# A graph-attention kernel: GpSimd's semaphore add at the head of each gather group is taken out

## The chip, the cores and the metric

The kernel runs on one core of a Trainium2 chip. The metric is the device time of one execution in microseconds; the number given for a kernel is the median of its timed runs. A profile is one further execution, recorded by the hardware profiler; its span runs from the first to the last instruction.

The engines are TensorE (PE in the profile, with its weight loads as PEld), VectorE (DVE), ScalarE (ACT), GpSimd (POOL) and SyncE (SP). A name with a q behind it (POOLq, DVEq, SPq) is that engine's sequencer: waits, register work and the issue of transfers.

## The reference, cut to what matters

There are 6,250 nodes with 128 features and 206,250 edges, sorted by destination. Three products of the nodes are taken (Q, K, V), one of the edges (E). Each edge gets a score per head, and the messages are summed per destination:

```python
Qh = (h @ WQ).reshape(N, H, D)          # H = 8 heads, D = 16
Kh = (h @ WK).reshape(N, H, D)
Vh = (h @ WV).reshape(N, H, D)
Eh = (edge_attr @ WE).reshape(-1, H, D)
score = jnp.einsum('ehd,ehd,ehd->eh', Kh[src], Qh[dst], Eh) * inv_sqrt_d
score = jnp.exp(jnp.clip(score, -5.0, 5.0))
msg = Vh[src] * score[:, :, None]
wV = jax.ops.segment_sum(msg, dst, num_segments=N)
Z = jax.ops.segment_sum(score, dst, num_segments=N)
h_out = wV / (Z[:, :, None] + 1e-06)
x = _layernorm(x + h_out)
```

`Kh[src]` and `Vh[src]` are gathers of rows at random. The kernel does them with indirect transfers that GpSimd issues.

## The kernel before, in words

**Groups.** The edges are cut into 403 groups of 512 (G = 403, four tiles of 128 edges each). A first stage computes K and V of all nodes and writes them to `kv_table` in DRAM, and keeps Q on chip in three bf16 parts. The main loop then runs over the groups, eight to a turn; it is unrolled in full, so that each group has its own instructions.

**One group, engine by engine.**
- SP loads the group's 512 source indices into `src_idx` (L272) and its edge features into `attr` (L279). The index buffer has eight slots, `attr` four.
- GpSimd gathers the 512 rows of `kv_table` (1 KB each) into a ring of eight slots, `kv` (RINGS = 8), with four indirect transfers (L436), one for each tile.
- PE turns the edge features (L537, `attr_tr`), turns the one-hot matrix of destinations (L556, `hot_tr`), multiplies the features by WE (L546, `e_mm`), selects Q by the one-hot matrix (L569, `q_sel`) and sums the messages (L580, `sums`).
- ACT copies what PE turned out of PSUM (L726, L733), builds the one-hot matrix (L713, L718) and takes the exponential (L740).
- DVE multiplies K by E (L901, after `e_mm` and `kv_in`), by Q (L906), reduces to scores (L911), clips (L917), forms the messages (L923, `msg_ok`) and adds the sums to the accumulator (L940, after `sums`).

The engines are staggered: while DVE scores group g, PE turns g+2, makes the products of g+1 and sums the messages of g-1.

**The ring.** Group g of the gathers may overwrite its slot when the messages of group g-8 are made. This is the wait on `msg_ok`. The other wait of a group is that its indices have landed (`idx_in`). Both stand in the function `gather`, and behind them a semaphore `go` is raised by one. No instruction waits for `go`.

**Order.** Every engine runs its instructions in program order; what ties them together are the semaphores. After the last group the window sums that are still open are divided, added to x and normalised, and stored.

The names that the steps below touch are: `gather` (L429), its waits at L431 and L433, the add to `go` at L434, the gather itself at L436, and for comparison DVE's two waits ahead of L901 (`e_mm` written first, L898; `kv_in` second, L899) and PE's two ahead of L537 (`attr_in` first, L533; `attrT_ok` second, L535).

Of the kernel before, what the change touches and what calls it, by code (L numbers as in the profile page):

```python
# [32 lines left out]
def past(g, n):  # L33

    return g >= n if isinstance(g, int) else True


def graph_attention_layernorm(nc, x, src, dst, edge_attr, wq, wk, wv, we, out):
# [43 lines left out]
    def edge0(g):  # L82

        return min(g * GROUP, n_edges - GROUP) if isinstance(g, int) else g * GROUP
# [3 lines left out]
    with ExitStack() as ctx:  # L88
# [6 lines left out]
        def sem(name):  # L95
            return ctx.enter_context(nc.semaphore(name))
# [101 lines left out]
        go = sem("go")  # L198
# [199 lines left out]
        @block.gpsimd  # L398
        def _(pool):
            nc.gpsimd.memset(ident[:, :], 0.0).then_inc(id_zero, 1)  # L400
            pool.wait_ge(id_zero, 1)
            nc.gpsimd.affine_select(out=ident[:, :], in_=ident[:, :], compare_op=ALU.not_equal, fill=1.0, base=0,
                                    pattern=[[-1, P]], channel_multiplier=1).then_inc(const_ready, 1)

            def count_up(out, base, n):
                return nc.gpsimd.iota(out, [[1, n]], base=base, channel_multiplier=0,
                                      allow_small_or_imprecise_dtypes=True)


            count_up(iota[:, 0, :], 0, P)  # L410
            count_up(iota[:, 1, 0:HALF], HALF, HALF)
            count_up(iota[:, 1, HALF:P], 0, HALF).then_inc(const_ready, 1)
            nc.gpsimd.iota(table[0:1, FIRST, 0:G - 1], [[GROUP, G - 1]], base=0, channel_multiplier=0)
            nc.gpsimd.iota(table[0:1, FIRST, G - 1:G], [[0, 1]], base=edge0(G - 1), channel_multiplier=0)\
                .then_inc(first_ok, 1)

            nc.gpsimd.iota(table[0:1, OPEN, 0:B_LAST * RINGS].rearrange("a (b u) -> a b u", u=RINGS),
                           [[2, B_LAST], [0, RINGS]], base=2 * (2 - LAG), channel_multiplier=0)
            nc.gpsimd.iota(table[0:1, OPEN, B_LAST * RINGS:G + 1], [[0, G + 1 - B_LAST * RINGS]], base=2 * EARLY,
                           channel_multiplier=0).then_inc(first_ok, 1)  # L420

            pool.wait_ge(prep, 4)
            last = local_rows[:, GC - 1, :]
            nc.gpsimd.affine_select(out=last, in_=last, compare_op=ALU.is_ge, fill=NOT_AN_EDGE,
                                    base=LAST_ROW * 2 * GROUP - REPEATED, pattern=[[1, GROUP]],
                                    channel_multiplier=-2 * GROUP).then_inc(masked, 1)
            nc.gpsimd.memset(acc[:, :, :], 0.0).then_inc(acc_zero, 1)

            def gather(b, u):  # L429
                g = b * RINGS + u  # L430
                pool.wait_ge(idx_in[u], b * 16 + 16)  # L431
                if past(g, RINGS):
                    pool.wait_ge(msg_ok, g - RINGS + 1)  # L433
                pool.sem_inc(go, 1)  # L434
                for t in range(TILES):
                    nc.gpsimd.indirect_dma_start(  # L436
                        out=kv[:, u, t, :], out_offset=None, in_=kv_table,
                        in_offset=bass.IndirectOffsetOnAxis(ap=src_idx[:, u, t:t + 1], axis=0)).then_inc(kv_in[u], 16)

            for i in range(RINGS):  # L440
                pool.wait_ge(kv_stored[i], 16 * len(range(i, CH, RINGS)))
            for u in range(RINGS):
                gather(0, u)
            for b in range(1, B_LAST):
                for u in range(RINGS):
                    gather(b, u)
            for g in range(B_LAST * RINGS, G):
                gather(g // RINGS, g % RINGS)


            pool.wait_ge(table_ok, 1)
            with pool.If(pool.value_load(table[0:1, STRAYS, G:G + 1], min_val=0, max_val=G) > 0):
                with pool.Fori(0, G) as g:
                    nth = pool.value_load(table[0:1, STRAYS, bass.ds(g, 1)], min_val=0, max_val=G)
                    nth_next = pool.value_load(table[0:1, STRAYS, bass.ds(g + 1, 1)], min_val=0, max_val=G)
                    with pool.If(nth_next > nth):
                        pool.wait_ge(s_idx, nth * 16 + 16)
                        pool.sem_inc(go, 1)
                        for t in range(TILES):
                            nc.gpsimd.indirect_dma_start(  # L460
                                out=kv[:, 0, t, :], out_offset=None, in_=kv_table,
                                in_offset=bass.IndirectOffsetOnAxis(ap=src_idx[:, 0, t:t + 1], axis=0))\
                                .then_inc(s_kv, 16)
# [649 lines left out]
```

## Time and profile before

| | us |
|---|---|
| median of 3 runs | 3040.36 |
| the runs | 3032.72 to 3042.60 |
| the profiled execution, device time | 3033.75 |
| its span, first to last instruction | 3031.9 |
| PE busy (share of the span) | 2078.2 (69%) |
| DVE busy | 1490.8 (49%) |
| ACT busy | 1331.4 (44%) |
| POOL busy, 1612 gathers 1530.9 of it | 1539.4 (51%) |
| TensorE's mean granted clock | 0.803 |

No engine is busy for the whole span, so the busy shares alone don't say what bounds the kernel: the order in which the engines wait for each other has to be read. "Issue" as a releaser means that the profile shows nothing that the engine waited for; "remote" and "another core or an unknown queue" mean that the semaphore came from an instruction that the inference did not find.

### The profile page before, as it was taken

To read this page: it belongs to the slowest core of one execution; us is meant where nothing else is said; L and a number is where in the kernel's file an instruction comes from. 1 tells how busy PE (TensorE), PEld (TensorE's weight loads), DVE (VectorE), ACT (ScalarE), POOL (GpSimd) and SP (SyncE) were. 2 spreads that over 40 slices of the span, in tenths; PEclk is the share of its full clock that TensorE was granted. 3 is DMA by queue.
4 is the path that set the end of the run, shared out by engine and by line. 5 is a ranking of instruction groups with operands and counts; after the bars stand their busy time and mean duration, and the time that the engine had idled before them with its cause. 6 is when DMAs were issued, how large, how long until landed. Compare 5 with 4: busy or idle time off the path is not lost.

```text
span 3031.9 us, 50000 instructions
## 1 busy us (share of the span) xinstructions
PE 2078.2 (69%) x14786; PEld 1828.8 (60%) x14787; DVE 1490.8 (49%) x3785; ACT 1331.4 (44%) x3270; POOL 1539.4 (51%) x1628
## 2 busy tenths in 40 slices
PE   6566766776766766667676776676666676767775
PEld 5455656666656665566666666566565566666665
DVE  4444444554454544544445544455445454454546
ACT  2444444444444444444444444444444444444443
POOL 3455554555555555555555555555554555545552
PEclk8688887878787788888777777878878888777778
DMA  7533433433333433334333443333333343433431
GB/s 218 158 110 109 114 111 108 115 111 109 110 110 108 113 111 110 111 109 113 109 111 110 112 112 110 112 106 111 114 109 109 110 112 112 110 110 107 116 109 55
DMA packets 223039, 342.94 MB, mean 113 GB/s; under 512 B 92096, under 2 KB 117672, under 8 KB 222779
## 3 DMA queue, kind: packets, MB, share of 16 engines
q0 software_dynamic: 77376, 211.39, 24.0%
q1 hardware_dynamic: 144827, 128.08, 15.5%
q8 instruction: 132, 2.16, 0.3%
q14 instruction: 128, 1.05, 0.1%
q10 hardware_dynamic: 576, 0.26, 0.0%
HBM read 325.24 MB, written 9.60 MB: 110 GB/s over the span
## 4 chain that ended last, share of the span: by engine, by line
PE 30%; another core or an unknown queue 28%; DVE 18%; issue 16%; DVEq 5%; ACT 3%; DMA 0%; SPq 0%; ACTq 0%
PE psW L580 13%; DVE msg L923 6%; PE psE L546 6%; DVE acc L940 4%; PE psH L556 4%; DVEq L246 3%; PE psQ L569 3%; DVE prod L906 2%; PE psT L537 2%; ACT hot L713 1%; DVE score L911 1%; DVEq L940 1%; ACT hot L718 1%; PE psE L499 1%
## 5 line engine op out<-in xcount | busy, mean ns | idle before, releaser
L436 POOL DMA_INDIRECT kv<-kv_table,src_idx x1612 | 1530.9, 950 | 1437.7 <-issue 1411.3
L580 PE MATMUL psW<-msg,hot 128*128 128x136 f32 x3224 | 647.7, 361 | 379.1 <-DVE msg L923 379.0
L580 PEld LDWEIGHTS psW<-msg,hot 128*128 128x128 f32 x3224 | 555.8, 252 | 419.4 <-DVE msg L923 419.1
L940 DVE TENSOR_TENSOR acc<-psW,acc 64x136 f32 x806 | 239.5, 297 | 1117.3 <-remote 938.8
L726 ACT ACTIVATE attrT<-psT 128x512 f32<-128x512 f32 x403 | 239.8, 595 | 964.9 <-remote 944.7
L569 PE MATMUL psQ<-Qp,hotT 128*128 x4836 | 422.4, 231 | 262.0 <-issue 261.3
L546 PE MATMUL psE<-w_e,attrT 128*128 128x128 f32 x3224 | 539.6, 308 | 89.4 <-issue 85.9
L569 PEld LDWEIGHTS psQ<-Qp,hotT 128*128 128x128 bf16 x4836 | 340.4, 104 | 360.4 <-issue 353.6
L546 PEld LDWEIGHTS psE<-w_e,attrT 128*128 128x128 f32 x3224 | 486.8, 225 | 81.4 <-issue 79.9
L713 ACT ACTIVATE hot<-iota,local 128x128 f32 x1612 | 508.8, 386 | 3.0 <-issue 2.6
L901 DVE TENSOR_TENSOR prod<-kv,psE 128x512 f32<-128x512 f32 x403 | 275.1, 683 | 327.3 <-issue 231.8
L556 PE MATMUL psH<-ident,hot 128*128 128x128 f32 x1612 | 326.3, 337 | 99.0 <-ACT hot L718 51.3
L537 PE MATMUL psT<-ident,attr 128*128 128x128 f32 x1612 | 329.0, 342 | 65.8 <-issue 65.8
L556 PEld LDWEIGHTS psH<-ident,hot 128*128 128x128 f32 x1612 | 219.4, 171 | 199.0 <-ACT hot L718 134.2
L740 ACT ACTIVATE msg<-clipped 128x32 f32<-128x32 f32 x403 | 92.4, 229 | 535.5 <-DVE clipped L917 457.4
L537 PEld LDWEIGHTS psT<-ident,attr 128*128 128x128 f32 x1612 | 263.4, 181 | 74.6 <-issue 74.6
L718 ACT ACTIVATE hot<-hot,one 128x512 f32<-128x512 f32 x403 | 290.9, 722 | 13.0
L906 DVE TENSOR_TENSOR prod<-prod,psQ 128x512 f32<-128x512 f32 x403 | 277.2, 688 | 12.7
L733 ACT ACTIVATE hotT<-psH 128x512 bf16<-128x512 f32 x403 | 239.6, 595 | 90.9 <-PE psH L556 80.4
L923 DVE TENSOR_TENSOR msg<-kv,msg 128x512 f32<-128x512 f32 x403 | 275.9, 685 | 0.3 <-ACT msg L740 0.3
L911 DVE TENSOR_REDUCE score<-prod 128x32 f32<-128x512 f32 x403 | 270.6, 671 | 0.0
L917 DVE TENSOR_SCALAR clipped<-score 128x32 f32<-128x32 f32 x403 | 76.6, 190 | 4.6
(94 smaller groups left out, 362.2 us busy)
## 6 DMA issues: line engine op xcount, KB each, us to landing
attr<-in_edge_attr_dram SPq DMA_DIRECT2D x403, 256.0 KB
kv<-kv_table,src_idx POOLq DMA_INDIRECT x1612
src_idx<-in_src_dram SPq DMA_DIRECT2D x403, 2.0 KB
kv_table<-kv SPq DMA_DIRECT2D x12, 512.0 KB, 3.8
Qp<-Qp SPq DMA_DIRECT2D x23, 192.0 KB
hot<-in_x_dram SPq DMA_DIRECT2D x12, 256.0 KB, 4.5
xT<-in_x_dram SPq DMA_DIRECT2D x8, 384.0 KB
out_dram<-xT SPq DMA_DIRECT2D x45, 64.0 KB
```

The lines of the kernel that those rows point to most:

```text
L436: nc.gpsimd.indirect_dma_start(out=kv[:, u, t, :], out_offset=None, in_=kv_table, in_offset=bass.IndirectOffsetOnAxis(ap=src_idx[:, u, t:t ...
L537: last = nc.tensor.transpose(psT[:, t * P:(t + 1) * P], attr[:, u % ATTRS, t, :], ident[:, :])
L546: last = nc.tensor.matmul(psE[:, u % 2, t * P:(t + 1) * P], attrT[:, u % 2, t * P:(t + 1) * P], w_e[:, :], start=True, stop=True)
L556: last = nc.tensor.transpose(psH[:, t * P:(t + 1) * P], hot[:, g % HOTS, t, :], ident[:, :])
L569: last = nc.tensor.matmul(psQ[:, u % 2, t * P:(t + 1) * P], hotT[:, u % 2, t * P:(t + 1) * P], Qp[:, bass.ds(slot, 1), part, :].rearrange( ...
L580: last = nc.tensor.matmul(psW[:, u % 2, 0:MW], hot[:, g % HOTS, t, :], msg[:, g % MSGS, t, :], start=(t == 0), stop=(t == TILES - 1))
L713: last = nc.scalar.activation(hot[:, g % HOTS, t, :], nodes, ACT.Abs, scale=-1.0, bias=local[:, t, bass.ds(g, 1)])
L718: nc.scalar.activation(slot, slot, ACT.Relu, scale=-1.0 / NOT_AN_EDGE, bias=one[:, 0:1])\
L906: nc.vector.tensor_tensor(prod[:, :], prod[:, :], psQ[:, u % 2, :], ALU.mult).then_inc(keq, 1)
L911: nc.vector.tensor_reduce(score[:, :], prod[:, :].rearrange("p (a d) -> p a d", d=DH), AX.X, ALU.add)\
L923: nc.vector.tensor_tensor(per_head(msg[:, g % MSGS, :, 0:dim]), per_head(kv[:, u, :, dim:2 * dim]), msg[:, g % MSGS, :, dim:MW].unsqueeze( ...
L940: last = nc.vector.tensor_tensor(where, psW[half, u % 2, 0:MW], where, ALU.add)
```

## The change

The line that adds to `go` is removed from `gather`. The two waits ahead of it stay in the program, and so does the order of the four gathers behind them. Nothing else changes; the add in the branch for stray edges at the end of GpSimd's program stays, and that branch isn't entered with these inputs.

```diff
@@ -431,7 +431,6 @@
                 pool.wait_ge(idx_in[u], b * 16 + 16)
                 if past(g, RINGS):
                     pool.wait_ge(msg_ok, g - RINGS + 1)
-                pool.sem_inc(go, 1)
                 for t in range(TILES):
                     nc.gpsimd.indirect_dma_start(
                         out=kv[:, u, t, :], out_offset=None, in_=kv_table,
```

In the program before, both waits are carried by the instruction that adds to `go`, an EVENT_SEMAPHORE of GpSimd's sequencer at L434. Without it the next instruction behind the waits is the group's first gather.

## Rows read from the trace of the kernel before

**Rows 1.** The page's costliest gather line: busy, mean ns, idle before, releaser.
```profile
L436 POOL DMA_INDIRECT kv<-kv_table,src_idx x1612 | 1530.9, 950 | 1437.7 <-issue 1411.3
```

**Rows 2.** Waits of all engines: who waited for whom, us, times, longest.
```profile
POOL kv L436 <- issue: 1411.3, 1611, 34.5
ACT attrT L726 <- remote: 944.7, 197, 5.9
DVE acc L940 <- remote: 938.8, 197, 7.1
```

**Rows 3.** Stretches: length, each engine's busy us (instructions), clock, DMA share, GB/s.
```profile
1508.01:1522.53 14.52, 10.97 (x74) 9.40 (x74) 7.48 (x22) 6.47 (x16) 7.60 (x8) 0.74 0.38 110
1522.53:1537.11 14.58, 11.14 (x74) 9.48 (x74) 7.14 (x21) 6.52 (x16) 7.56 (x8) 0.73 0.38 109
2990.00:3018.80 28.80, 21.68 (x191) 19.63 (x190) 21.73 (x50) 13.51 (x35) 0.00 (x0) 0.94 0.03 11
```

**Rows 4.** Timeline of GpSimd: start, duration, instruction, idle before and its releaser.
```profile
1508.01 0.95 POOL L436 DMA_INDIRECT kv<-kv_table,src_idx  x1 [5.05 <-issue]
1509.26 0.94 POOL L436 DMA_INDIRECT kv<-kv_table,src_idx  x1 [0.30 <-issue]
...
1516.80 0.94 POOL L436 DMA_INDIRECT kv<-kv_table,src_idx  x1 [0.30 <-issue]
1522.53 0.94 POOL L436 DMA_INDIRECT kv<-kv_table,src_idx  x1 [4.79 <-issue]
```

**Rows 5.** Timeline of ACT and DVE behind that burst.
```profile
1519.53 0.60 ACT L726 ACTIVATE attrT<-psT 128x512 f32<-128x512 f32 x1 [4.41 <-remote]
...
1521.07 0.68 DVE L923 TENSOR_TENSOR msg<-kv,msg 128x512 f32<-128x512 f32 x1
```

**Rows 6.** GpSimd's waiting instruction L434, whole run: duration ns min/median/max, first and last start.
```profile
L434 POOLq EVENT_SEMAPHORE  x403: 17/2973/11407, 52.4 to 2977.9; - x135
```

**Rows 7.** The same line in the stretches 53:95, 1513:1522.5 and 1523:1524.
```profile
L434 POOLq EVENT_SEMAPHORE  x7: 17/17/17, 54.4 to 74.2; - x7
...
L434 POOLq EVENT_SEMAPHORE  x1: 7934/7934/7934, 1513.9 to 1513.9; - x1
...
L434 POOLq EVENT_SEMAPHORE  x1: 2677/2677/2677, 1523.7 to 1523.7; - x1
```

**Rows 8.** Lines with two waits, on DVE and on PE: the rows that exist.
```profile
L899 DVEq EVENT_SEMAPHORE  x403: 4/21/174, 115.0 to 3011.5; - x135
...
L901 DVE TENSOR_TENSOR prod<-kv,psE x403: 672/681/690, 115.2 to 3011.6; 128x512 f32<-128x512 f32 x135
...
L535 PEldq EVENT_SEMAPHORE  x402: 51/51/51, 106.6 to 3003.7; - x134
```

**Rows 9.** SP's index loads: duration ns, first and last start; then GpSimd's last gathers.
```profile
L272 SPq DMA_DIRECT2D src_idx<-in_src_dram x403: 327/432/972, 4.3 to 2950.2; - x135
...
2981.74 0.94 POOL L436 DMA_INDIRECT kv<-kv_table,src_idx  x1 [0.30 <-issue]
2983.93 0.94 POOL L436 DMA_INDIRECT kv<-kv_table,src_idx  x1 [1.24 <-issue]
...
2986.42 0.95 POOL L436 DMA_INDIRECT kv<-kv_table,src_idx  x1 [0.30 <-issue]
```

**Rows 10.** Timeline of GpSimd at the start: the first burst's ends and the next gather.
```profile
53.30 1.11 POOL L436 DMA_INDIRECT kv<-kv_table,src_idx  x1 [34.51 <-issue]
...
93.47 0.95 POOL L436 DMA_INDIRECT kv<-kv_table,src_idx  x1 [0.30 <-issue]
120.79 0.94 POOL L436 DMA_INDIRECT kv<-kv_table,src_idx  x1 [26.38 <-DVE msg L923]
```

**Rows 11.** Timeline of GpSimd: a burst with a pause inside, and the next.
```profile
1537.11 0.94 POOL L436 DMA_INDIRECT kv<-kv_table,src_idx  x1 [4.89 <-issue]
...
1542.11 0.94 POOL L436 DMA_INDIRECT kv<-kv_table,src_idx  x1 [0.30 <-issue]
1544.30 0.94 POOL L436 DMA_INDIRECT kv<-kv_table,src_idx  x1 [1.24 <-issue]
...
1549.88 0.94 POOL L436 DMA_INDIRECT kv<-kv_table,src_idx  x1 [2.14 <-issue]
```

## The prediction

> **What bounds the kernel now.** I read the page first. GpSimd's gathers take 1530.9 us, with almost as much idle time between them that no releaser explains [rows 1]. So GpSimd isn't saturated on average, and the question is what its gaps are. The list of waits comes next: ACT and DVE each wait 197 times, some 940 us in all, for something that PE raises (the turned features, the sums), and the releaser isn't found [rows 2]. 403 groups over 197 such waits is two groups a wait, so there is a cycle of two groups. The stretches show it: one cycle is 14.52 to 14.58 us long and holds 8 gathers and 74 matmul records. In the tail, after the last gather, 191 matmul records take 28.80 us. At 37 records a group that is 5.2 groups, so a group takes 7.3 us with gathers in flight and 5.6 without [rows 3]. The clock differs too (0.74 against 0.94).
>
> The timeline gives the cycle's parts. A burst of eight gathers starts at 1508.01 at a pitch of 1.25 us and ends at 1516.80 + 0.94 = 1517.74 [rows 4]. ACT's copy of the turned features, which had waited 4.41 us, starts at 1519.53, and DVE's messages, begun at 1521.07, are ready at 1521.75 [rows 5]. They free a ring slot, and the next burst starts at 1522.53 [rows 4]. So the cycle is
>
> 9.73 (burst) + 1.79 (last gather's end to ACT's release) + 2.22 (to the messages) + 0.78 (to the first gather) = 14.52 us.
>
> PE's semaphores come late in each burst, and come when the burst has drained; why, the trace doesn't say. What matters here is that GpSimd's own time lies on the loop: whatever the head of a burst gains or loses counts once per cycle, 197 times. The span is then 120.8 us to the first gather that waits for messages [rows 10], 2866.6 us of cycles up to 2987.4 [rows 9], and 44.5 us of tail, 3031.9 in all.
>
> **The head of a group before.** The instruction that adds to `go` carries both waits. There is one in each of the 403 groups [rows 6]. In the burst above it stands from 1513.9 for 7.934 us, so it ends at 1521.8, when the messages are ready, and the gather starts 0.7 us behind it [rows 7, 4]. The next one starts at 1523.7, behind four gathers: the sequencer passed four in 1.9 us, 0.47 us each, while the engine needs 1.25 each. So the sequencer runs ahead within a burst, and only the first gather of a burst shows its 0.7 us of start. When both conditions hold already the whole instruction takes 17 ns [rows 7].
>
> **The change, part by part.**
>
> *The add itself.* Nobody waits for `go`. Its cost lies between 0 and the whole satisfied instruction, 17 ns [rows 7]. On 197 burst heads that is 0 to 3.3 us of gain; the other 206 heads are passed while earlier gathers run, and are hidden by them. If that cover were gone they would cost 206 x 0.017 = 3.5 us more.
>
> *Where the waits go.* DVE has two waits ahead of L901. The one written second, `kv_in` at L899, has an EVENT_SEMAPHORE of its own, 403 times; the one written first has no row, so L901 carries it. PE's pair ahead of L537 looks the same: a row at L535, the second [rows 8]. By this pattern GpSimd's second wait, the ring slot, stays an EVENT_SEMAPHORE (now at L433), and the first gather carries the index wait. This is the main point of the forecast: the wait that really ends late, the slot's, still blocks the sequencer before the gather is read, and the 0.7 us of start behind it stay. Only in the first eight groups, which have one wait, the instruction disappears: 8 x 0.017 us, at a time when GpSimd is 26.38 us early [rows 10].
>
> *The wait that the gather now carries.* Queued behind it are the other three gathers of the group and all later ones, and DVE's L901 waits for them. It is satisfied long before: the last index load is issued at 2950.2, and the four gathers of the last group begin at 2981.74 or later, over 31 us behind it [rows 9]. What a carried, satisfied wait costs on a gather no row shows. From below I exclude a gain, since it adds a check. From above I take the dearest satisfied wait by median, PE's 51 ns [rows 8]; DVE's is 21 ns, GpSimd's own 17 [rows 7, 8]. The 51 ns belong to another engine, so I take 17 ns: 197 x 0.017 = 3.3 us, with 0 and 197 x 0.051 = 10.0 as ends. Heads inside a burst are again covered by the gathers that run.
>
> *Sum.* 3033.75 - 3.3 + 3.3 = 3033.75 us for an execution like the profiled one, with ends 3030.4 and 3043.8. That execution lies 6.6 us under the median of the runs, 3040.36. Moved by that, the forecast is 3040.4 us, from 3037.1 to 3050.4; the runs before themselves spread by 10 us, so I widen the case to 3031 at the low end. A change of up to 0.3% (9.1 us) can't be told from none for this kernel.
>
> **A rule of the skill on the carried wait.** The row for GpSimd says that a satisfied wait passes in 17 ns [rows 7]. The Trainium skill, "Advanced Engine Details and Errata", section Miscellaneous Facts, gives 50 to 100 ns for a sequencer's reading of a semaphore. If each burst head paid one such reading more, that would be an estimate of 197 x 0.05 to 0.1 = 10 to 20 us more, 3050 to 3060 us. The trace's satisfied waits, at 17 and 21 ns, don't agree with it.
>
> **The rivals.**
>
> 1. *The ring-slot wait rides on the gather (faster).* If a transfer can carry both waits, or the slot's is the one it carries, the sequencer has read the gather before the slot is free. No row shows a transfer with two waits, so the profile doesn't exclude it; the pattern of two other engines speaks against it [rows 8]. Price: a start like one inside a burst, 0.30 us of gap instead of about 0.74, or one gather's 0.47 us of reading saved: 197 x 0.44 to 0.47 = 87 to 93 us [rows 4, 7]. Then 2948 to 2954 us. What is late next is unchanged, the same loop with a shorter head. The Trainium skill, "Perfetto Trace Analysis", section DMA Instruction — SWDGE (GPSIMD), says that such an instruction is pushed into a wait queue and the sequencer goes on to the next: by that rule, the gain is there whenever the gather carries the slot's wait.
>
> 2. *A gather that carries a wait isn't run ahead (slower).* No row of this trace shows a GpSimd transfer with a wait. If the sequencer reads such a gather only when the one before has ended, the fifth gather of each burst, now hidden, gets the gap of a burst's head: 0.74 instead of 0.30 us, 197 x 0.44 = 87 us, 3127 us. It decides as soon as the carried wait is handled after the read-ahead rather than in it. Against it: the program's other engines carry a wait in every group and run on.
>
> 3. *A small price for each carried wait (slower).* Satisfied waits at PE's 51 ns would give 10.0 us, and twice that 20: 3050 to 3061 us [rows 8].
>
> 4. *A pause inside the burst lets PE through (faster).* One burst in the trace has a pause of 1.24 us behind its fifth gather, and its cycle is 1549.88 - 1537.11 = 12.77 us, shorter by 1.75 than the one shown above, though GpSimd lost 0.94 us [rows 11, 3]. If the carried wait opened such a gap in every burst, 197 x 1.75 = 345 us would go: 2696 us. Nothing says that the gap would be that long.
>
> That the change doesn't do what it says, since the waiting instruction stays, is part of the forecast.
>
> **How the numbers follow.** The forecast, within 0.3%, gets 0.68. Rival 1 gets 0.10, rival 2 0.06, rival 3 0.10, rival 4 0.02; 0.04 is left for what I don't see, half to each side. So faster is 0.10 + 0.02 + 0.02 = 0.14, the same 0.68, slower 0.06 + 0.10 + 0.02 = 0.18. The likeliest case has the range 3031 to 3050. With rival 3, up to 3061, it holds 0.78, just short of 8 in 10, so the range goes down to rival 1 as well, to 2945, and holds 0.88; rivals 2 and 4 are left out.
>
> **What would show each step.** In the profile of the changed kernel: an EVENT_SEMAPHORE of GpSimd at L433, 395 times, with durations like L434's now, and none in the first eight groups (the placement); the first gather of a burst still 0.7 to 0.8 us behind the messages, and the others at a pitch of 1.25 us (the head); the cycle at 14.5 us and 197 waits of ACT for PE (the loop). The prediction is wrong if there is no such instruction and the head's 0.78 us have shrunk (rival 1), if the gap before the fifth gather of a burst is over 0.30 us (rival 2, or 4 if the cycle is then shorter), or if the head grows by 0.05 us or more (rival 3).

## The result and the profile after

| | before | after |
|---|---|---|
| median of 15 runs each, us | 3037.55 | 3030.35 |
| lowest to highest | 3024.01 to 3042.99 | 3020.01 to 3033.79 |
| profiled execution, us | 3033.75 | 3031.2 |
| its span | 3031.9 | 3029.4 |

The ratio is 0.9978, with a 95% interval from 0.9969 to 0.9987. By that ratio the change gives 6.7 us, between 3.9 and 9.4 (the medians are 7.2 apart). The forecast said that nothing would be gained or lost, with 3.3 us as the most that the add could give. A gain was measured, small, but clear of the noise.

The page's line for the gathers and the list of waits, as in [rows 1] and [rows 2] (busy, mean ns and idle in the page's line; us, times and longest in the waits):

```profile
L435 POOL DMA_INDIRECT kv<-kv_table,src_idx x1612 | 1534.2, 952 | 1430.7 <-DVE msg L922 960.9
```
```profile
DVE acc L939 <- remote: 979.6, 196, 7.0
POOL kv L435 <- DVE msg L922: 960.9, 259, 27.2
ACT attrT L725 <- remote: 938.7, 198, 6.1
```

The loop is the same: ACT and DVE wait 196 to 198 times for PE, 939 and 980 us in all. Only the name of GpSimd's releaser is new. Before, the wait lay in the long record of the adding instruction; now the gather is shown to wait for the messages. The waiting instruction over the whole run, to be held against [rows 6] (duration ns min/median/max, first and last start):

```profile
L433 POOLq EVENT_SEMAPHORE  x395: 17/17/17, 121.6 to 2977.3; - x198
```

It stands at L433, 395 times, and not in the first eight groups. Its place was foreseen. Its durations were not: all are 17 ns, at the time when the wait ends, where the old one's record held the wait (2973 ns median). The record of such an instruction says when it ran, but not what it costs. The forecast took its price from such a record.

One burst and the head of the next in the timelines of DVE and GpSimd, to be read beside [rows 4] and [rows 5]:

```profile
1516.53 0.68 DVE L922 TENSOR_TENSOR msg<-kv,msg 128x512 f32<-128x512 f32 x1
```
```profile
1503.47 0.95 POOL L435 DMA_INDIRECT kv<-kv_table,src_idx  x1 [5.03 <-DVE msg L922]
1504.73 0.94 POOL L435 DMA_INDIRECT kv<-kv_table,src_idx  x1 [0.30 <-issue]
...
1508.81 0.95 POOL L435 DMA_INDIRECT kv<-kv_table,src_idx  x1 [0.30 <-issue]
...
1512.55 0.94 POOL L435 DMA_INDIRECT kv<-kv_table,src_idx  x1 [0.30 <-issue]
1517.97 0.94 POOL L435 DMA_INDIRECT kv<-kv_table,src_idx  x1 [4.47 <-DVE msg L922]
```

The messages are ready at 1517.21 and the burst starts at 1517.97, 0.76 us later by these rounded rows. The fifth gather (1508.81), which carries a wait inside the burst, still has its gap of 0.30 us.

Worked out for every burst head in the trace, this distance is so steady that single nanoseconds can be read: 775 ns before and 751 ns after, nine heads in ten within 1 ns. That is 24 ns less in each of 197 heads, 4.7 us. The cycles took 2866.6 us before; after, from 122.3 to the last gather's end at 2984.0, they take 2861.8, 4.8 less. The start (+1.5) and the tail (+0.9) give a part back in this execution. The interval of the 6.7 us holds 4.7. But the agreement is closer than the parts: the regular cycles of eight gathers became 46 ns shorter on average (14.621 to 14.575 us), not 24, which is 9 us, and the few irregular ones, most with a pause like that of [rows 11], saved 12.9 us in all instead of 17.1. So the 24 ns of the head are measured, and that they are all of the gain is not.

### The profile page after: what moved, and what is told of

Its sections match the earlier page's. It is cut to its first block, busy times and chain, and to the rows that moved or that the text cites. A ratio compares the mean times of both kernels' runs of the same rounds, so it can differ in the third digit from the quotient of the medians.

```text
span 3029.4 us, 49992 instructions
## 1 busy us (share of the span) xinstructions
PE 2066.5 (68%) x14786; PEld 1815.6 (60%) x14787; DVE 1492.3 (49%) x3785; ACT 1331.8 (44%) x3270; POOL 1542.7 (51%) x1628
## 3 DMA queue, kind: packets, MB, share of 16 engines
q1 hardware_dynamic: 144827, 128.08, 15.8%
## 4 chain that ended last, share of the span: by engine, by line
PE 34%; another core or an unknown queue 23%; issue 18%; DVE 17%; DVEq 4%; ACT 3%; DMA 0%; SPq 0%; ACTq 0%
PE psW L579 14%; PE psE L545 7%; DVE msg L922 6%; PE psH L555 5%; PE psQ L568 5%; DVE acc L939 3%; PE psT L536 3%; DVEq L246 3%; DVE prod L905 2%; ACT hot L712 2%; DVE score L910 1%; ACT hot L717 1%; DVEq L939 1%; PE psE L498 1%
## 5 line engine op out<-in xcount | busy, mean ns | idle before, releaser
L568 PE MATMUL psQ<-Qp,hotT 128*128 x4836 | 429.8, 230 | 299.0 <-issue 298.3
L545 PE MATMUL psE<-w_e,attrT 128*128 128x128 f32 x3224 | 524.9, 307 | 41.2 <-issue 37.8
L545 PEld LDWEIGHTS psE<-w_e,attrT 128*128 128x128 f32 x3224 | 480.3, 225 | 39.4 <-issue 38.6
```

The lines of the kernel that those rows point to most:

```text
L545: last = nc.tensor.matmul(psE[:, u % 2, t * P:(t + 1) * P], attrT[:, u % 2, t * P:(t + 1) * P], w_e[:, :], start=True, stop=True)
L568: last = nc.tensor.matmul(psQ[:, u % 2, t * P:(t + 1) * P], hotT[:, u % 2, t * P:(t + 1) * P], Qp[:, bass.ds(slot, 1), part, :].rearrange( ...
```

## The experiments

The theory to be tested, A: GpSimd's time in a burst's head counts once a cycle, and the add was 24 ns of it. The rivals: the 24 ns come from the new place of the waits; or the head doesn't set the time at all.

The runs fell on chips of two kinds. On the kind of the first measurement the kernel before takes 3035 to 3076 us and gathers in bursts. On the other kind it takes 2125 to 2130 us, with no bursts. Each result names the kernel before on the same chip. Edits are shown against the kernel before where nothing else is said.

### e1_swap: which wait the gather carries

```diff
-                pool.wait_ge(idx_in[u], b * 16 + 16)
                 if past(g, RINGS):
                     pool.wait_ge(msg_ok, g - RINGS + 1)
+                pool.wait_ge(idx_in[u], b * 16 + 16)
-                pool.sem_inc(go, 1)
```

> The add is gone and the two waits are written in the other order, so that the sequencer's own waiting instruction holds the index wait (long satisfied) and the first gather carries the ring-slot wait. Theory A (the burst head's time is mostly the reading of the gather behind the waiting instruction): the first gather starts about 0.3 us behind the messages instead of 0.75, which takes 197 x 0.44 = 87 us away: near 2945 us. Theory B (the sequencer handles a carried wait itself, before it reads the gather): the head stays at 0.75 us or so and the time is that of the changed kernel, near 3030 us.

Measured: 2993.61 us, before 3075.99, ratio 0.9736 (0.9723 to 0.9749). The head, in DVE's timeline and then GpSimd's:

```profile
1514.03 0.68 DVE L922 TENSOR_TENSOR msg<-kv,msg 128x512 f32<-128x512 f32 x1
```
```profile
1514.99 0.94 POOL L435 DMA_INDIRECT kv<-kv_table,src_idx  x1 [4.09 <-DVE msg L922]
```

1514.71 to 1514.99: 270 ns over all heads, in place of 775. When the gather carries the wait that ends last, most of GpSimd's start lies ahead of it and is no longer paid. How far ahead the sequencer is, the row of the index wait shows (stretch 1514 to 1515.1):

```profile
L433 POOLq EVENT_SEMAPHORE  x1: 17/17/17, 1514.8 to 1514.8; - x1
```

It ends 0.07 us behind the messages and 0.2 us before the gather starts, and by its semaphore it is the index wait of the group behind this one. So the sequencer had passed all four gathers of the group before the slot was free.

The head fell by 505 ns, 99.5 us in 197 cycles, and 82.4 us came out. Other parts moved too (medians, against e2 and e4 below, which ran on the same chip): the fourth gather of a burst takes 1.18 us in place of 0.95, the time from the last gather's end to ACT's release is 1.86 us in place of 2.00, and the bursts with a pause are gone. Why, no run shows. It is faster than both kernels.

### e2_add_first, e3_two_adds, e4_add_behind: where an add stands and how many

```diff
 e2_add_first
+                pool.sem_inc(go, 1)
                 pool.wait_ge(idx_in[u], b * 16 + 16)
...
-                pool.sem_inc(go, 1)
 e3_two_adds
                 pool.sem_inc(go, 1)
+                pool.sem_inc(go, 1)
 e4_add_behind
-                pool.sem_inc(go, 1)
                 for t in range(TILES):
+                    if t == 1:
+                        pool.sem_inc(go, 1)
```

> The add to go stands ahead of both waits: the work is that of the kernel before, but no add lies between the slot's release and the gather. Theory A (the changed kernel's 24 ns are the add on the head of a burst): head 0.751 us as in the changed kernel, ratio to before about 0.998. Theory B (they are the price of one instruction more, or of the semaphore traffic, wherever it stands): head 0.775 us, ratio 1.000.

Measured: 3079.43 us, before 3075.99, ratio 1.0009 (1.0000 to 1.0018). The head is 755 ns.

> The kernel before with a second add to go behind the first, on the head of every group. Theory A (what stands between the release and the gather counts once per burst): the head grows from 0.775 us by the time of one more sequencer instruction, 0.03 to 0.09 us, and the time by 197 times that, 6 to 17 us, ratio 1.002 to 1.006. Theory B (the head of a burst is not on the loop; the changed kernel's gain comes from elsewhere): the head may grow, the time stays, ratio 1.000.

Measured: 3088.12 us, ratio 1.0044 (1.0031 to 1.0058). The head is 853 ns. DVE's and GpSimd's timelines, then the rows of the two adding instructions over the whole run (duration ns min/median/max, first and last start):

```profile
1518.50 0.69 DVE L924 TENSOR_TENSOR msg<-kv,msg 128x512 f32<-128x512 f32 x1
```
```profile
1520.04 0.94 POOL L437 DMA_INDIRECT kv<-kv_table,src_idx  x1 [5.23 <-issue]
```
```profile
L434 POOLq EVENT_SEMAPHORE  x403: 17/2897/11504, 51.5 to 3028.9; - x135
L435 POOLq EVENT_SEMAPHORE  x403: 17/17/17, 51.6 to 3031.6; - x135
```

> The add to go stands between a group's first and second gather; the waits are as in the changed kernel. Theory A (only what stands on the head counts): head 0.751 us, ratio to before 0.998, like the changed kernel. Theory B (an add anywhere in the group costs): ratio 1.000.

Measured: 3068.89 us, ratio 0.9982 (0.9973 to 0.9991). The head is 755 ns.

What follows. A second add, with its row of 17 ns, costs 78 ns in the head: 15.4 us in 197 cycles, and 12.1 were measured in the medians. This speaks for the head being on the loop, and shows that a row's 17 ns isn't its price. e4 behaves like the changed kernel, in head and time. e2 is the miss: its head is as short as e4's, yet nothing was gained. Their regular cycles are 14.73 and 14.72 us (median). They differ in the few bursts that have a pause inside, like that of [rows 11]: these took 14.38 us for eight gathers in e2's profile and 14.17 in e4's. Against a regular cycle these bursts save 6.5 us in e2's profile and 12.0 in e4's, a difference as large as the whole effect. Why they differ stays open, and with it how much of the 6.7 us is the head's: two programs with the same head are 10.5 us apart. An add ahead of the waits, or behind the first gather, is nearly free in the head: 755 ns in e2 and e4, against 751 with none. Only between the last wait and the gather does a second one cost 78 ns.

### e5_add_one_wait and e6_three_waits: the add or the wait

e5 moves the wait for the next group's indices to this group's second gather; the head keeps the add, with the slot's wait alone. e6 has no add, and a third wait that has always been met.

```diff
 e5_add_one_wait
-                pool.wait_ge(idx_in[u], b * 16 + 16)
+                if g == 0:
+                    pool.wait_ge(idx_in[u], b * 16 + 16)
...
+                    if t == 1 and g + 1 < G:
+                        pool.wait_ge(idx_in[(u + 1) % RINGS], (b + (u + 1) // RINGS) * 16 + 16)
 e6_three_waits
+                    pool.wait_ge(kv_stored[0], 16)
-                pool.sem_inc(go, 1)
```

> The wait for a group's indices is moved to the second gather of the group before, so that GpSimd's head of a group is one instruction: the add, which itself carries the only wait left, the one for the ring slot; the gather behind it carries none. From the messages' end to the burst's first gather the kernel before takes 775 ns, the changed one 751 ns. Theory A (the 24 ns are the add: one more instruction between the wait and the gather, whatever it carries): the add is there and the head stays at 775 ns, 0.3% (some 5 us) off the kernel before at most. Theory B (the 24 ns are the second wait: the one behind which an instruction of its own has to stand): the head falls to 751 ns or below, the cycle by the same. Rival C (a satisfied wait carried by a gather costs time of its own, and the add costs more than 24 ns): the head falls below 740 ns, as the gather is free of any wait.

> No add; the head of a group waits for three things instead of two, in the order indices, ring slot, and a first store of the table that has long landed; the gather carries the first, the others stand ahead of it. It measures what one more wait that is already satisfied costs in the head. Theory A (an extra wait that is satisfied is one more instruction in the way, priced as the add is): the head from the messages' end to the first gather is 751 + 24 to 40 = 775 to 790 ns, the cycle of two groups 0.02 to 0.04 us above the changed kernel's 14.55 us, the time 4 to 8 us above it. Rival B (satisfied waits are taken together with the one that ends last and cost nothing): 751 ns and the changed kernel's time. By the second add's price (78 ns) it would be 829 ns.

Measured, both on the kind without bursts: 2132.43 and 2130.28 us, one run each, before 2129.89. There the gathers never stop, and no head is to be seen (e6, timeline of GpSimd):

```profile
1503.19 0.95 POOL L436 DMA_INDIRECT kv<-kv_table,src_idx  x1 [0.30 <-issue]
1504.45 0.95 POOL L436 DMA_INDIRECT kv<-kv_table,src_idx  x1 [0.31 <-issue]
1505.70 0.94 POOL L436 DMA_INDIRECT kv<-kv_table,src_idx  x1 [0.30 <-issue]
```

They ran again on the kind with bursts.

> The same kernel as e5_add_one_wait, which ran on a chip where GpSimd's gathers never stop (0.305 us between two gathers throughout, 2132 us), so that no head of a burst was to be seen. On a chip where the kernel before takes over 3000 us and its gathers come in bursts of eight: Theory A (the 24 ns are the add) 775 ns from the messages' end to the burst's first gather; Theory B (the 24 ns are the second wait) 751 ns or less; Rival C (a carried satisfied wait costs more) below 740 ns. On a chip of the other kind it shows again 0.305 us and the time of the kernel before, whatever stands in the head.

> The same kernel as e6_three_waits (no add, a third wait that is always satisfied). On a chip with bursts: Theory A (an extra satisfied wait is one more instruction in the way) 775 to 790 ns from the messages' end to the first gather and 4 to 8 us over the changed kernel; Rival B (satisfied waits cost nothing) 751 ns. On a chip without bursts: 0.305 us between gathers and the time of the kernel before.

Measured: 3031.09 and 3031.30 us, before 3035.28, one run each; the times can't be told apart, the heads can. e5b's and e6b's, DVE and then GpSimd each:

```profile
1516.51 0.68 DVE L926 TENSOR_TENSOR msg<-kv,msg 128x512 f32<-128x512 f32 x1
```
```profile
1517.97 0.95 POOL L439 DMA_INDIRECT kv<-kv_table,src_idx  x1 [4.52 <-DVE msg L926]
```
```profile
1519.15 0.69 DVE L923 TENSOR_TENSOR msg<-kv,msg 128x512 f32<-128x512 f32 x1
```
```profile
1520.57 0.96 POOL L436 DMA_INDIRECT kv<-kv_table,src_idx  x1 [4.75 <-issue]
```

Neither theory named what came: 785 ns for e5b, 739 ns for e6b. With the two older kernels they make a table in which every entry is the sum of the same two parts (medians, ns; in brackets from the messages' end to the end of the head's last instruction, and from there to the gather):

| the head's instruction | carries two waits | carries one wait |
|---|---|---|
| with an add | before: 775 (41 + 733) | e5b: 785 (52 + 733) |
| without | e6b: 739 (41 + 698) | after: 751 (53 + 698) |

The step from the upper row to the lower is worth 35 ns, all of it behind the instruction. An instruction with one wait answers 11 to 12 ns later than one with two. The change of this case does both: 35 ns gained, 12 lost (775 to 751; the rounding takes the last one). A satisfied third wait makes the head no longer here.

One thing the table doesn't take apart: in the upper row the gather carries no wait, in the lower it carries the index wait. The 35 ns are the add's price less whatever that wait costs on the gather. The add so costs 35 ns or more.

### e9_thin: is it the gathers' data?

Why is there a cycle of 14.5 us at all? In the changed kernel's profile PE's turned features are done long before ACT is released (timelines of PE and ACT):

```profile
1511.30 0.60 PE L536 MATMUL psT<-ident,attr 128*128 128x128 f32 x4
```
```profile
1514.99 0.60 ACT L725 ACTIVATE attrT<-psT 128x512 f32<-128x512 f32 x1 [5.28 <-remote]
```

PE ends at 1511.90 and ACT starts at 1514.99, 3.1 us later, when the burst has drained. The same pair on the other kind of chip (e6):

```profile
1500.67 0.60 PE L537 MATMUL psT<-ident,attr 128*128 128x128 f32 x4
```
```profile
1501.30 0.60 ACT L726 ACTIVATE attrT<-psT 128x512 f32<-128x512 f32 x1
```

0.03 us. The semaphore events in the traces say the same of all that PE raises: in e6 its sums are posted 0.01 us after the matmul's end, all of them. In e1 this holds for one group of each pair; the other's are posted 5.27 us late (median of 198). ACT's and DVE's own posts come after 0.01 us in both. e9 is e1 with narrow rows: it leaves out 15/16 of every row.

```diff
 e9_thin (against e1_swap)
-                        out=kv[:, u, t, :], out_offset=None, in_=kv_table,
+                        out=kv[:, u, t, 0:16], out_offset=None, in_=kv_table.rearrange("n (a d) -> (n a) d", d=16),
```

> As e1_swap, but each gather moves 16 of a row's 256 numbers, from a narrow view of the table: 15/16 of the gathered bytes are left out, and the result is not the reference's. The number of gathers and of their rows, and with them the work of GpSimd in writing descriptors, stay. Theory M (TensorE's posts are held back by the data that the gathers move): with 1/16 of the bytes the posts come through, the gathers no longer come in bursts, the time falls to that of a kernel bound by GpSimd, 2000 to 2150 us. Theory G (they are held back by GpSimd's writing of descriptors, whatever the bytes): bursts of eight and a cycle of 14 us or a little less, 2850 to 2990 us. On a chip without bursts: 0.305 us between gathers, 1.25 us a gather, 2000 to 2130 us by either theory.

Measured: 2959.34 us, before 3035.28 (one run each). The stretch from 1500 to 1600 us shows how little moves (the last two columns are the DMA engines' share and GB/s; e1_swap moves 113 to 115 GB/s in its cycles):

```profile
1500.00:1600.00 100.00, 70.78 (x510) 62.25 (x510) 51.06 (x133) 45.94 (x113) 55.28 (x57) 0.81 0.19 45
```

The bursts of eight stay, the cycle is 14.13 us against 14.31, and the later group's sums are still posted 4.81 us late. So the bytes don't hold PE's posts. What is left is GpSimd's issue of the gathers, as theory G has it, or the number of rows that the transfers handle, which the edit left as it was; no run separates the two.

### e8_pause, e8b_pause, e8c_short: a pause inside the burst

e1 with two small clears of an unused tile on GpSimd, each waiting for the one before, behind every other group's first gather.

```diff
                 for t in range(TILES):
+                    if t == 1 and g % 2 == 0 and g >= RINGS:
+                        for i in range(2):
+                            n = (g - RINGS) // 2 * 2 + i
+                            if n:
+                                pool.wait_ge(go, n)
+                            nc.gpsimd.memset(stray[:, :], 0.0).then_inc(go, 1)
```

> As e1_swap, with a pause written into each burst of 8 gathers behind its fifth gather: two small clears of an unused tile on GpSimd, each waiting for the one before. Theory A (GpSimd's work in a cycle is on the path and adds up): the cycle of 14.31 us grows by what the clears and the pause take, 0.3 to 0.8 us, the time from 2994 to 3050 to 3150 us. Rival (the fourth rival of the prediction: in the pause TensorE's posts, held back while gathers stream, come through, and the chain of the next pair of groups starts earlier; the few bursts with a pause in the kernel before have cycles of 13.8 us per eight gathers, against 14.6): the cycle falls to 13.0 to 13.8 us, the time to 2700 to 2900 us.

Measured without bursts: 2312.74 us, before 2129.89, ratio 1.0856 (1.0831 to 1.0880). GpSimd is the bound there, and pays for the clears.

> The same kernel as e8_pause, which on a chip without bursts took 8.6% more than the kernel before: the two clears take 1.9 us of GpSimd per pair of groups. On a chip with bursts: Theory A (GpSimd's work in a cycle is on the path and adds up): 14.31 + 0.9 to 1.9 = 15.2 to 16.2 us a cycle, 3170 to 3370 us. Rival (in the pause TensorE's held posts come through and the chain of the next pair starts earlier): 12.8 to 13.8 us, 2700 to 2900 us, though GpSimd has more to do.

Measured with bursts: 2910.77 us, before 3035.28 (one run each), 4.1% less, with more work on GpSimd. The gathers now come in groups of many sizes, 13.9 us for eight. Of the 393 posts of PE's sums in its trace 97 fall between two gathers that have the clears between them. The fourth rival of the prediction has its mechanism here.

> As e8b_pause, with the two clears cut to 8 numbers a row each, so that they take little time of their own. On a chip with bursts, Theory P with any pause enough: as much or more gain than e8b (4.1%), 2850 to 2910 us. Rival (the pause of the clears must be long, some 1.1 us between two gathers, for the posts to come through): no gain beyond e1_swap's 2.6%, 2950 to 3010 us. On a chip without bursts: less lost than e8's 8.6%, 0 to 3%.

e8c clears 8 numbers a row in place of 403. Measured with bursts: 2935.58 us, before 3036.8, ratio 0.9674 (0.9652 to 0.9696). The pause, in GpSimd's timeline:

```profile
1507.79 0.95 POOL L441 DMA_INDIRECT kv<-kv_table,src_idx  x1 [0.30 <-issue]
1508.73 0.29 POOL L440 MEMSET stray<- 128x8 bf16 x2
1509.16 0.95 POOL L441 DMA_INDIRECT kv<-kv_table,src_idx  x1
```

It is 0.42 us between two gathers, against 0.30 without it, and even this gives a little over e1's 0.9736, which was measured on another chip. I had expected either the full 4% or nothing; it lies between.

### e7_sums_gate, e7b_sums_gate, e10_gate_even: a stop until PE has posted

```diff
 e7_sums_gate (against e1_swap)
-                    pool.wait_ge(msg_ok, g - RINGS + 1)
+                    pool.wait_ge(sums, g - RINGS + 1)
 e10_gate_even (against e1_swap)
-                    pool.wait_ge(msg_ok, g - RINGS + 1)
+                    pool.wait_ge(msg_ok if g % 2 else sums, g - RINGS + 1)
```

> As e1_swap (no add, the gather itself carries the wait for the ring slot), but the slot is taken as free by the counter of the sums that follow the messages and not by that of the messages themselves. The gathers of a burst so begin later after the messages by what stands between the two in VectorE's and TensorE's order. Theory A (the cycle is the plain sum of burst, release, messages and head; a later release is paid in full): the cycle grows by that distance, 2.2 us if the sums end a group's chain later, 14.3 to 16.5 us, the time to 3400 us. Rival (with later gathers the semaphore posts of TensorE that are now held until the last gather's data land come out sooner, and the groups no longer come in pairs): bursts of 4 in place of 8, and the cycle of two groups falls below 14.3 us, the time to 2700 to 2950 us.

Measured without bursts: 2131.47 us, before 2129.89, ratio 1.0005 (0.9993 to 1.0018).

> The same kernel as e7_sums_gate, which on a chip without bursts took the time of the kernel before (1.0005); on a chip with bursts every group's gathers wait for the sums of the group 8 before. Theory A: the later release is paid in full, 14.3 to 16.5 us a cycle, to 3400 us. Theory P (a stop of GpSimd lets TensorE's posts out): bursts of four, 2760 to 2990 us; it should come out above e10_gate_even, since the burst's first gather starts later as well.

Measured with bursts: 2555.43 us (two runs), before 3036.8, ratio 0.8421 (0.8401 to 0.8441). This beats every forecast made for it. Timeline of GpSimd, and the stretch from 600 to 1000 us in e7b and in the kernel before (busy time of PE, PEld, DVE, ACT, POOL; clock, DMA share, GB/s):

```profile
1501.32 0.94 POOL L435 DMA_INDIRECT kv<-kv_table,src_idx  x1 [1.30 <-remote]
1502.57 0.95 POOL L435 DMA_INDIRECT kv<-kv_table,src_idx  x1 [0.30 <-issue]
1503.82 0.95 POOL L435 DMA_INDIRECT kv<-kv_table,src_idx  x1 [0.30 <-issue]
1505.08 0.95 POOL L435 DMA_INDIRECT kv<-kv_table,src_idx  x1 [0.31 <-issue]
1507.35 0.94 POOL L435 DMA_INDIRECT kv<-kv_table,src_idx  x1 [1.32 <-remote]
```
```profile
600.00:1000.00 400.00, 268.87 (x2387) 242.02 (x2387) 235.84 (x623) 213.71 (x534) 253.48 (x265) 0.95 0.47 133
```
```profile
600.00:1000.00 400.00, 279.01 (x1963) 244.63 (x1961) 195.72 (x513) 177.91 (x439) 206.94 (x220) 0.80 0.39 110
```

GpSimd stops for 1.3 us (median) behind nearly every four gathers, until PE's sums are posted, and the post of the turned features comes out some 0.06 us behind (median). A group takes 6.0 us, eight gathers 12.1 in place of 14.3 in e1. The granted clock is 0.95 of the full level (2.4 GHz) in this stretch and 0.80 in the same stretch before, though PE was busy for 268.87 us here and for 279.01 there: at the higher clock it did 2387 matmul records in less time than the kernel before did 1963. So a part of the gain may be the clock's and not the stop's. How large it is, and why the clock is higher, no run takes apart.

> As e1_swap, but the even groups, whose first gather is the fifth of a burst, wait for the sums of the group 8 before (a post of TensorE) instead of its messages (a post of VectorE); the odd ones, which open a burst, wait for the messages as before. On a chip with bursts, Theory P (TensorE's posts are held while gathers stream and come out as soon as there is a pause, which is why e8b gained 4.1% with more work on GpSimd): GpSimd now stops after four gathers until the post is out, bursts of four, 13.2 to 13.9 us for eight gathers, 2760 to 2900 us, and nothing lost on a chip without bursts (within 0.3% of the kernel before). Theory A (the chain of release, messages and sums is simply paid later): the wait adds up to 2.2 us to a cycle of 14.31 us, up to 3430 us.

Measured: 3122.82 us, before 3036.8, ratio 1.0299 (1.0276 to 1.0322). I had expected a gain. The gate was meant for the fifth gather of a burst. But the bursts shifted by one group:

```profile
1509.41 0.95 POOL L435 DMA_INDIRECT kv<-kv_table,src_idx  x1 [0.30 <-issue]
1515.16 0.95 POOL L435 DMA_INDIRECT kv<-kv_table,src_idx  x1 [4.80 <-PE psW L579]
```

Now the gated group opens the burst, 2.51 us behind the messages in place of 0.27, and the ungated one follows with no stop. The later start is paid and no pause is had: theory A's case. The gate has to stand in every group.

### e11_before_sums, e12_after_sums, e13_two_stops

e11 is the kernel before with `sums` in the place of `msg_ok`, e12 the changed kernel with the same. e13 is e7 with a second stop ahead of the third gather.

```diff
 e11_before_sums, e12_after_sums
-                    pool.wait_ge(msg_ok, g - RINGS + 1)
+                    pool.wait_ge(sums, g - RINGS + 1)
 e13_two_stops (against e7_sums_gate)
+                    if t == 2 and past(g, RINGS):
+                        pool.wait_ge(q_sel, g - RINGS + 4)
```

> The kernel before with one word changed: the slot is free by the counter of the sums, not of the messages; the add and the order of the waits are those of the kernel before. It takes e7b_sums_gate (2555 us) apart into the gate and the order. Theory P (stops after each group's four gathers let TensorE's posts out; that is the whole gain): it keeps the stops and pays the long head, some 0.5 us in each of 395 groups, 200 us at most: 2560 to 2760 us. Rival (the short head is needed for the stops to pay): 2950 us or more. On a chip without bursts: the time of the kernel before by either.

> The change of this case made in e11_before_sums: its add at the head is gone, the rest stands. If each group now has a head of its own and it is on the path in full, 24 ns in each of 395 groups: 9.5 us (0.35%) below e11. If the pause in front of a group's gathers is covered by other engines' work: 0 to 3 us. On a chip without bursts: no difference.

> As e7b_sums_gate, with a second stop in each group: the third gather waits for a q select of TensorE (that of the group 5 before), the next post but some that TensorE makes behind the sums. Theory P in its plain form (the more often GpSimd stops, the earlier the posts come): below 2555 us. Rival D (a post comes out with the landing of the gathers' data, some 1.2 us after the last gather's end, so that each stop costs that much whatever it lets out): two stops of 1.3 us and 4.7 us of gathers, 7 us a group in place of 6.0, some 2900 us. On a chip without bursts: within 0.3% of the kernel before.

Measured, all on a chip without bursts: 2128.76, 2130.02 and 2128.95 us, before 2125.02, ratios 1.0019 (1.0004 to 1.0034), 1.0019 (1.0003 to 1.0036) and 1.0023 (1.0009 to 1.0036). e12 takes the add out of e11 and gains nothing: while the gathers follow each other without a stop, the head is hidden, with its add and its waits. e11 holds one more row, of the adding instruction with its two waits, here both met at most heads (whole run, duration ns min/median/max):

```profile
L434 POOLq EVENT_SEMAPHORE  x403: 17/43/7339, 52.8 to 2086.7; - x135
```

The 17 ns are those of the first groups, which have one wait; with two met waits the record is 43 ns. What e7b's 15.8% owes to the short head, and what a second stop does, can't be read from these runs and stay open. Where there are no bursts the gates cost 0.05% (e7) to 0.2%.

## Why the prediction was wrong, point by point

- **The loop: right.** Start, 197 cycles and tail add up in both profiles. e3 and e1, by +78 and -505 ns in the head and +12.1 and -82.4 us in time, speak for the head counting once a cycle. e2 doesn't: its head is 20 ns shorter and its time is not. Effects of a few microseconds are within what the bursts with a pause can give or take.
- **Where the waits go: right.** The slot's wait kept an instruction of its own at L433, 395 times; the gather took the index wait.
- **The carried wait on the gather: not measured apart.** The 3.3 us set against the add stood for the gather's check. What the runs show in that place is 2.4 us (12 ns x 197), and it comes from the slot's wait standing alone on its instruction. What the gather's check costs is inside the 35 ns below.
- **The add: this step failed.** The prediction put it "between 0 and the whole satisfied instruction, 17 ns", from the 17 ns row [rows 7]. That reading is wrong twice. The seven instructions of that row start at 54.4 to 74.2 us, in the first eight groups, which have one wait and not both, and where both are met the record is 43 ns (e11). And the record holds the instruction's own time; what it delays behind it is in no row. Without the add the distance from the head's last instruction to the gather is 35 ns shorter (e5b against after, e6b against before), 6.9 us in 197 heads. The two netted terms of 3.3 us are -6.9 and +2.4, -4.5 us; the direct count gives -4.7. With 35 or 43 ns as the add's upper end the sum's lowest value would have held the measured gain of 6.7. The low end of the case was widened by the spread of the runs and not by the term that was unsure, and the chance for "no difference" was too high for a sum whose terms were both guessed at 17 ns.
- **Rival 1, the slot's wait on the gather: not what this change does, and priced well in part by luck.** 87 to 93 us were worked out, e1 gives 82. But the head fell by 505 ns and not by 440 to 470, and a longer fourth gather, an earlier release of ACT and the missing pauses, none of them foreseen, made up the rest. The rule of the Trainium skill, "Perfetto Trace Analysis", section DMA Instruction — SWDGE (GPSIMD), that the sequencer goes on once such an instruction is in the wait queue, agrees with e1's 270 ns and with the next group's index wait, which ran before the gather started.
- **Rival 2, no running ahead: fell.** The fifth gather carries a wait and has 0.30 us before it.
- **Rival 3, a price for each carried wait: fell.** The rule of the Trainium skill, "Advanced Engine Details and Errata", section Miscellaneous Facts, of 50 to 100 ns for reading a semaphore, isn't borne out as a price of one more satisfied wait: e6b's third one moves the head by -12 ns. What the wait on the gather itself costs isn't measured apart, but the head as a whole got shorter and not longer.
- **Rival 4, a pause lets PE through: didn't happen with this change, but the mechanism is real.** e8b, e8c and e7b show it, worth 3% to 16% against the kernel before, the 2.6% of e1's order included.

## What to carry over

A semaphore instruction on a loop can cost more than its row (35 and 78 ns here, for rows of 17 to 43): set it beside a kernel without it, and read the distance between the event that releases it and the work behind it. If an indirect transfer has two waits, write the one that ends last first, so that the transfer carries it; the start of the transfer then lies ahead of the wait (-2.6% here, one line moved). And where semaphores of one engine come late and in bunches while another issues transfers, a stop on one of these semaphores in every group can gain more than any trimming: 15.8% on a chip with bursts, about nothing on one without.

## What the runs showed of the hardware

- **Two kinds of chip.** The kernel before takes 3035 to 3076 us on one and 2125 to 2130 on the other. TensorE's mean granted clock is 0.803 in the profile of the first and 0.979 in e6's. The difference is there from the first groups on. From 53 to 94 us both issue the same first gathers, and the stretches show what the other engines do meanwhile (after, then e6; busy time of PE, PEld, DVE, ACT, POOL, then clock, DMA share, GB/s):

```profile
53.00:94.00 41.00, 15.35 (x95) 13.43 (x95) 12.36 (x19) 10.52 (x19) 30.57 (x31) 0.67 0.71 172
```
```profile
53.00:94.00 41.00, 22.13 (x144) 19.11 (x143) 28.19 (x42) 22.78 (x47) 31.13 (x31) 0.79 0.95 231
```

  DVE does 12.4 us of work in one and 28.2 in the other, with GpSimd equally busy. On the first kind PE's semaphores are posted up to some 6 us late while gathers are issued; on the second 0.01 us. Of the gathers' 25,792 completions (sixteen a gather) the trace before records 6,732, e6's 25,432. Those recorded on the first kind come three or four to a gather and then in a bunch as the burst drains; what becomes of the others isn't shown. What makes a chip of one kind or the other no run shows.
- **A head that a transfer's wait removes.** Messages to first gather: 270 ns with the slot's wait on the gather, 739 to 785 ns with it on an instruction ahead, 853 with a second add behind it. The distances are worked out from the traces, as medians over the heads.
- **One wait or two.** An instruction with two waits, one of them long met, ended 41 ns behind the messages, one with a single wait 52 to 53.
- **Where a wait shows.** With two waits on it the instruction's record lasts as long as the wait, as in [rows 6] and in e6b's row (whole run, duration ns min/median/max), and 43 ns where both are met. With one it is 17 ns, as in the changed kernel, and the wait is found at the gather behind it.

```profile
L434 POOLq EVENT_SEMAPHORE  x395: 1219/3630/45602, 78.2 to 2974.6; - x198
```
